# Softplus and the query mask on PSUM operands, feed-forward scales in the activation, the scan's source on GpSimd

## The chip, the cores and the metric

One core of one Trainium2 chip runs the whole program. The metric is the device time of one execution in microseconds; below that stand the span of the profiled execution (first to last instruction) and the granted TensorE clock. Everything is float32.

## The reference, cut to what matters

One decoder layer over 16 sequences of 64 tokens, width 128: a Mamba block (selective scan with 256 inner channels and 16 states), a cross attention with squared, L2-normalised scores (16 heads of 8), and a feed-forward of five scaled linear layers, each followed by a residual sum and a layer norm.

```python
xc = silu(causal_depthwise_conv(xm, conv_w, conv_b))
delta = jax.nn.softplus(dt @ W_dt + b_dt)
# for each token t: A is -exp(A_log), 256 channels x 16 states
h = jnp.exp(d_t[..., None] * A) * h + (d_t * u_t)[..., None] * B_t[:, None, :]
y = jnp.einsum('bdn,bn->bd', h, C_t)
...
qn = _l2_rownorm(q)
kn = _l2_rownorm(k)
scores = jnp.einsum('bhqd,bhkd->bhqk', qn, kn)
attn = scores * scores
...
h = jax.nn.silu(_tlin(x, w1_w, w1_s)) * _tlin(x, w2_w, w2_s)   # _tlin: (x @ w.T) * s, s per output column
h = jax.nn.gelu(_tlin(h, h1_w, h1_s), approximate=False)
h = jax.nn.gelu(_tlin(h, h2_w, h2_s), approximate=False)
return _tlin(h, w3_w, w3_s)
```

## The kernel before

The 1024 tokens are cut into four blocks (0 to 3) of 256. Channels or features lie on the 128 partitions and tokens along the free dimension, so a 256-channel tensor of a block is 128 x 2 x 256. Each engine works through a fixed list of steps, written out in `ORDER` (lines 86 to 144); a step is named `kind:block`, `kind:scan step` or the like, and an engine does its steps strictly in that order, waiting on semaphores inside each. So one late step holds all that stands behind it on its engine.

The selective scan is 32 scan steps, eight for each block, two states each. For step s: ScalarE writes the decays exp(delta*A) to PSUM (`decay_`, L897); GpSimd multiplies `du` (delta times the input) by B (`scan_in`, L1228); VectorE runs the recurrence (`scan`, L1091); GpSimd multiplies by C (`scan_out`, L429, in `out_product`). For blocks 0 and 1 TensorE sums the products (`mamba_sum`, L653), for blocks 2 and 3 VectorE does (`reduce`, L1108). Then `mamba_y` (L1141, L1145) applies the gate, and the block goes on through `gate_out`, `proj_out`, norm 1, the attention (`query`, `attend`, `attend_out`, `attn_out`), norm 2, and the feed-forward (`gate_up`, `hid1`, `hid2`, `down`, L745, L760, L771) and norm 3. B and C are written to DRAM as rows (`bc_store`) and fetched back broadcast over the partitions (`b_fetch`, `c_fetch`), by SyncE's DMA queue.

The places that the change touches:

- Softplus, stably, as max(v,0) + log(1+exp(-|v|)) with a correction for the rounding of 1+e. ScalarE writes |v| to `expo` in SBUF (L873), then exp(-|v|) over it (L879), then the log into the PSUM tile that held v (L882). VectorE computes `pre` = max(v,0) (L1064), then `rest` from `expo` by L1072 (one SBUF input) and L1074 (`expo` and `rest`, two SBUF inputs), then L1080 with the log from PSUM. `soft_end` on VectorE then writes `delta` (L406) and `du` = delta * xc (L410), each with two SBUF inputs.
- Query mask: ScalarE copies q with its bias to SBUF (L948), squares it (L951), and VectorE multiplies the SBUF copy by a head mask, 128 x 4 x 256 (`mask_queries`, L437).
- Scales: four rows of 512 are broadcast into `hid_a` and `hid_b` by two DMAs (`late:1`, L469). `fold:0` multiplies two of them into w1T and w2T (L1043, L1044); `fold:1` and `fold:2` multiply the other two into h1T and h2T (L1047, 128 x 2048 each). `gelu_layer` on ScalarE (L984) takes 512 columns in one instruction.
- Small scaled matrices: a diagonal of d_skip (L1032, two instructions) and the scaled centring matrix (L1037), both on VectorE.

Of the kernel before, what the change touches and what calls it, by code (L numbers as in the profile page):

```python
# [33 lines left out]
MASK_ON = ("dve", "dve", "dve", "dve")  # L34
# [23 lines left out]
        ("d_skip", CH), ("b_out_bo", 2), ("bq", 1), ("bk", 1), ("s3", 1), ("hmask", HI), ("early", SEQS * (TAPS - 1)), ("eps", 2)]  # L58
# [3 lines left out]
def columns(parts):  # L62
    at, n = {}, 0
    for name, w in parts:
# [11 lines left out]
    "front": (("xm",), ("delta",), ("bc",), ("soft",), ("soft_end",)),  # L76
# [16 lines left out]
        gate_up:0:0 gate_up:0:1 gate_out:1 key_norm:1 hid1:0:0 proj_out:1 norm_var:1:1 values:1 keys:2 query:1
        hid1:0:1 query_norm:1 attend:1:0 hid2:0:0 attend:1:1 hid2:0:1 attend_out:1 key_norm:2 gate_out:2 attn_out:1
        norm_var:1:2 down:0 norm_var:0:3 keys:3 gate_up:1:0 gate_up:1:1 proj_out:2 hid1:1:0 norm_var:2:1 hid1:1:1
        query:2 values:2 query_norm:2 hid2:1:0 attend:2:0 hid2:1:1 attend:2:1 gate_z:3 attend_out:2 attn_out:2
        key_norm:3 norm_var:2:2 down:1 gate_out:3 norm_var:1:3 proj_out:3 norm_var:3:1 gate_up:2:0 gate_up:2:1
        values:3 query:3 hid1:2:0 query_norm:3 attend:3:0 hid1:2:1 attend:3:1 hid2:2:0 attend_out:3 attn_out:3
        hid2:2:1 norm_var:3:2 down:2 norm_var:2:3 gate_up:3:0 gate_up:3:1 hid1:3:0 hid1:3:1 hid2:3:0 hid2:3:1 down:3
        norm_var:3:3  # L100
    """,
    "act": """
        prep xm:0 prep2 delta:0 soft:0 decay:0 decay:1 keys:0 xm:1 xm:2 decay:2 decay:3 delta:1 prep3 soft:1 decay:4
        decay:5 decay:6 gate_m:0 delta:2 soft:2 decay:7 centre_w decay:8 decay:9 decay:10 decay:11 xm:3 gate_m:1
        gate_m:2 gate_z:1 gate_z:0 decay:12 decay:13 delta:3 norm_var:0:1 soft:3 decay:14 norm_scale:0:1 query:0
        query_norm:0 decay:15 decay:16 keys:1 attend:0:0 skip:2 attend:0:1 decay:17 decay:18 norm_var:0:2
        norm_scale:0:2 decay:19 gate_m:3 gate_z:2 gate_up:0:0 gate_up:0:1 decay:20 decay:21 decay:22 hid1:0:0
        norm_var:1:1 norm_scale:1:1 keys:2 query:1 decay:23 hid1:0:1 query_norm:1 attend:1:0 decay:24 hid2:0:0
        attend:1:1 hid2:0:1 decay:25 decay:26 norm_var:1:2 decay:27 norm_scale:1:2 norm_var:0:3 norm_scale:0:3
# [10 lines left out]
        scan:10 mamba_y:0 fold:1 gate_out:0 scan:11 bc:3 scan:12 delta:3 soft:3 norm_apply:0:1 scan:13 scan:14  # L120
        query:0 values:0 scan:15 scan:16 soft_end:3 attend_out:0 scan:17 fold:2 norm_apply:0:2 mamba_y:1 scan:18
        scan:19 gate_up:0:0 gate_up:0:1 scan:20 scan:21 key_norm:1 gate_out:1 reduce:6 norm_apply:1:1 scan:22
        values:1 query:1 scan:23 reduce:7 reduce:8 mamba_y:2 scan:24 key_norm:2 attend_out:1 scan:25 scan:26
        gate_out:2 norm_apply:1:2 norm_apply:0:3 scan:27 gate_up:1:0 gate_up:1:1 reduce:9 norm_apply:2:1 scan:28
# [100 lines left out]
def decoder_layer(nc, xT, ctxT, mats, vecs, bv, cw, srow, scratch, out):  # L225
# [11 lines left out]
    with ExitStack() as ctx:  # L237
# [107 lines left out]
        def tile(key):  # L345
            return bank[home[key]]
# [956 lines left out]
```

## Time and profile before

| | us |
|---|---|
| median of three runs | 263.56 (263.06 to 264.9) |
| the profiled execution's own time | 262.27 |
| its span, first to last instruction | 260.4 |
| mean granted TensorE clock in it | 0.937 |

Times of single instructions come from that one profiled execution. Each engine has a row of its own; "idle before, releaser" is how long the engine stood still in front of an instruction and what ended it. A group's mean hides its spread where an instruction sometimes has to wait inside.

### The profile page before, as it was taken

The page shows a single profiled execution, that of the slowest core. Times are in us where ns is not written, and L with a number is a line of the kernel's source. Part 1 is how long each engine was busy: PE and PEld are TensorE (multiplying, and loading weights), DVE is VectorE, ACT ScalarE, POOL GpSimd, SP SyncE. Part 2 cuts the span into 40 slices and gives each one's busy share as a digit, 9 for nine tenths or more (in the row PEclk, how much of TensorE's full clock was granted, in tenths as well). Part 3 has the DMA queues.
Part 4 walks back from the last instruction along what each step waited for, and adds up shares of the span by engine and source line. Part 5 has one row for each costly group of instructions (what it writes and reads, how often), then busy time and mean ns, then how long its engine had stood idle before and what let it go on. Part 6 is the DMA issues. An engine that isn't in the chain of part 4 may idle for free.

```text
span 260.4 us, 3882 instructions
## 1 busy us (share of the span) xinstructions
PE 223.2 (86%) x1458; PEld 158.4 (61%) x1458; DVE 180.0 (69%) x153; ACT 160.3 (62%) x310; POOL 160.2 (62%) x71
## 2 busy tenths in 40 slices
PE   8999709956999967889869798899899899988992
PEld 6777404534667433348737577687667677776881
DVE  1234899999997989988989999799996250004000
ACT  4077925493858855719885869899874728154113
POOL 4004999699959999999999499999460000000000
PEclk9999976996899997599985999999999999999998
DMA  6749235962400540523314422350000000000000
GB/s 216 290 131 316 84 145 167 392 268 84 142 24 0 166 161 1 159 86 113 133 59 137 130 81 83 72 193 2 0 3 0 24 0 3 3 0 20 0 3 20
DMA packets 7269, 25.44 MB, mean 98 GB/s; under 512 B 977, under 2 KB 1746, under 8 KB 7122
## 3 DMA queue, kind: packets, MB, share of 16 engines
q1 hardware_dynamic: 7250, 25.18, 28.0%
q8 instruction: 12, 0.20, 0.3%
q14 instruction: 7, 0.06, 0.1%
HBM read 24.52 MB, written 0.66 MB: 97 GB/s over the span
## 4 chain that ended last, share of the span: by engine, by line
PE 33%; DVE 22%; issue 17%; POOL 14%; ACT 7%; DMA 5%; SPq 0%; DVEq 0%; POOLq 0%; ACTq 0%
PE work L760 13%; DVE state L1091 8%; POOL prod L429 7%; POOL state L1228 7%; PE work L563 4%; ACT L792 3%; DVE qmask L437 3%; DMA b_buf<-bc_scratch 2%; DVE rest L1074 2%; DMA cw_row<-cw 2%; PE work L653 2%; DVE prod L1108 2%; PE work L710 2%; PE work L686 2%; PE work L670 1%
## 5 line engine op out<-in xcount | busy, mean ns | idle before, releaser
L1228 POOL TENSOR_TENSOR state<-du,b_buf 128x1024 f32<-128x1024 f32 x32 | 82.1, 2586 | 19.7 <-DMA b_buf<-bc_scratch 19.7
L429 POOL TENSOR_TENSOR prod<-state,c_buf 128x1024 f32<-128x1024 f32 x32 | 76.4, 2407 | 12.4 <-DVE state L1091 6.0
L1091 DVE TENSOR_TENSOR_SCAN state<-decay,state 128x1024 f32<-128x1024 f32 x32 | 72.1, 2276 | 6.4 <-POOL state L1228 4.5
L897 ACT ACTIVATE decay<-delta,neg_a 128x252 f32<-128x252 f32 x128 | 52.5, 459 | 15.6 <-DVE state L1091 13.5
L653 PE MATMUL work<-prod,mat 128*128 128x512 f32 x64 | 35.0, 691 | 10.3 <-DVE mat L1032 7.8
L792 ACT ACT_TABLE_LOAD x31 | 39.8, 1283 | 1.3 <-PEq L1296 0.7
L760 PE MATMUL work<-hid_a,mat 128*128 128x256 f32 x128 | 30.3, 391 | 1.1 <-DVE hid_a L1201 0.9
L760 PE MATMUL work<-hid_b,mat 128*128 128x256 f32 x128 | 29.3, 383 | 0.0
L653 PEld LDWEIGHTS work<-prod,mat 128*128 128x128 f32 x64 | 13.5, 220 | 25.5 <-issue 12.3
L760 PEld LDWEIGHTS work<-hid_a,mat 128*128 128x128 f32 x128 | 24.8, 197 | 5.7 <-issue 1.7
L760 PEld LDWEIGHTS work<-hid_b,mat 128*128 128x128 f32 x128 | 23.9, 190 | 4.8 <-issue 1.5
L1108 DVE TENSOR_REDUCE prod<-prod 128x512 f32<-128x4096 f32 x4 | 17.6, 4412 | 2.0 <-POOL prod L429 2.0
L563 PE MATMUL work<-x,wf 128*128 128x256 f32 (+3 forms) x64 | 17.9, 428 | 0.2 <-DVE bf L1015 0.2
L1166 DVE TENSOR_TENSOR final<-work,root_ffn 128x256 f32<-128x256 f32 x4 | 1.7, 424 | 22.5 <-ACT root_ffn L942 22.5
L745 PE MATMUL work<-x,mat 128*128 128x256 f32 x64 | 15.1, 383 | 0.2 <-DVE final L1166 0.2
L563 PEld LDWEIGHTS work<-x,wf 128*128 128x128 f32 x64 | 13.3, 217 | 2.6 <-DMA x<-xT 0.7
L984 ACT ACTIVATE hid_a<-work 128x512 f32<-128x512 f32 x8 | 4.8, 597 | 14.5 <-PE work L760 14.5
L745 PEld LDWEIGHTS work<-x,mat 128*128 128x128 f32 x64 | 11.9, 190 | 2.7 <-issue 0.6
L437 DVE TENSOR_TENSOR qmask<-q,vec 128x1024 f32<-128x1024 f32 x4 | 13.3, 3334 | 0.0
L710 PE MATMUL work<-qmask,keys 32*64 32x256 f32 x128 | 8.8, 389 | 3.5 <-DVE qmask L437 2.4
L984 ACT ACTIVATE hid_b<-work 128x512 f32<-128x512 f32 x8 | 4.8, 596 | 11.4 <-PE work L760 11.4
L1189 DVE TENSOR_TENSOR mat<-work,rq 128x128 f32<-128x128 f32 x8 | 1.9, 277 | 14.1 <-PE work L726 14.1
(134 smaller groups left out, 327.6 us busy)
## 6 DMA issues: line engine op xcount, KB each, us to landing
b_buf<-bc_scratch SPq DMA_DIRECT2D x16, 512.0 KB, 4.1
c_buf<-bc_scratch SPq DMA_DIRECT2D x16, 512.0 KB, 4.0
mat<-mats SPq DMA_DIRECT2D x1, 2560.0 KB, 10.5
mat<-mats SPq DMA_DIRECT2D x1, 640.0 KB, 4.2
cw_row<-cw SPq DMA_DIRECT2D x1, 512.0 KB, 5.4
x<-xT SPq DMA_DIRECT2D x1, 512.0 KB, 6.2
kv<-ctxT SPq DMA_DIRECT2D x1, 512.0 KB, 8.1
hid_a<-srow SPq DMA_DIRECT2D x1, 512.0 KB, 11.3
```

The lines of the kernel that those rows point to most:

```text
L429: engine.tensor_tensor(products(b, n), slot(s), c_buf[c % C_RING][:, states, None, :].broadcast_to([P, SG, CH, T]), ALU.mult).then_inc(don ...
L437: engine.tensor_tensor(qmask[:, :, :], q[:, None, :].broadcast_to([P, HI, T]), v("hmask")[:, :, None].broadcast_to([P, HI, T]), ALU.mult). ...
L563: mm(o[:, :, late:], wf4[:, k, c * P:(c + 1) * P], xs[:, :, 0:SEQ - late], start=(late == 0), stop=False, skip_group_check=True)
L653: i = mm(tile(("y", b))[:, :], ident, products(b, n)[:, k, :, :].rearrange("p c t -> p (c t)"), start=(n == 0 and k == 0), stop=False, ski ...
L710: i = mm(tile(("s", b, g))[e * SEQ:(e + 1) * SEQ, p * HI * SEQ:(p + 1) * HI * SEQ], keysT[b % KEEP][r, t:t + SEQ], qmask[r, :, t:t + SEQ], ...
L745: i = mm(tile((key, b, j))[:, n * T:(n + 1) * T], m(w)[:, (2 * j + n) * P:(2 * j + n + 1) * P], x2[b % 2][:, :], start=True, stop=True)
L760: i = mm(tile((key, b, j))[:, n * T:(n + 1) * T], w[:, k, c:c + P], src[:, k, :], start=(k == 0), stop=(k == FT - 1))
L792: nc.scalar.preload_act_table_set(name)
L897: i = act_(decay[:, s % DA_RING, k, c, :].rearrange("p (s t) -> p s t", t=SEQ)[:, :, 1:], delta[b % KEEP][:, c, :].rearrange("p (s t) -> p ...
L1091: vec_.tensor_tensor_scan(h, decay[:, s % DA_RING, :, :, :].rearrange("p k c t -> p (k c t)"), h, 0.0, ALU.mult, ALU.add).then_inc(scanned, 1)
L1108: vec_.tensor_reduce(dst, src, axis=AX.XY, op=ALU.add).then_inc(reduced, 1)
L1228: nc.gpsimd.tensor_tensor(slot(s), du[b % KEEP][:, None, :, :].broadcast_to([P, SG, CH, T]), b_buf[c % B_RING][:, states, None, :].broadca ...
```

## The change

1. Softplus of blocks 1 to 3: exp(-|v|) goes into the PSUM tile that held v, not back to `expo` in SBUF, and L1072 and L1074 read it there. Since the log overwrites the same tile, ScalarE now waits for both of them before the log, and for `pre` before the exp. Block 0 stays as it was.
2. `soft_end` keeps only `delta`; `du` becomes a step of its own, on VectorE for block 0 and on GpSimd for blocks 1 to 3.
3. The query mask reads q from PSUM and adds the bias in the same VectorE instruction; ScalarE's SBUF copy of q is gone.
4. The scales of the second and third feed-forward layers are given to Gelu as per-partition scale, so each Gelu becomes two instructions of 256 columns; `fold:2` and both 2048-column products are gone (`fold:0` and `fold:1` now do w1T and w2T), and the second scale DMA too.
5. The diagonal and the scaled centring matrix are made on ScalarE (in `prep3`), not VectorE.
6. All five orders are written anew.

```diff
+DU_ON = ("dve", "pool", "pool", "pool")
...
+        def exponential(b):
+
+            return expo[:, :, :] if b == 0 else tile(("dl", b))[:, :].rearrange("p (c t) -> p c t", c=CH)
+
...
-            engine.tensor_tensor(delta[b % KEEP][:, :, :], pre[:, :, :], rest[:, :, :], ALU.add).then_inc(soft_step, 1)
-            eng.wait_ge(soft_step, 2 * b + 1)
+            engine.tensor_tensor(delta[b % KEEP][:, :, :], pre[:, :, :], rest[:, :, :], ALU.add).then_inc(delta_ready, 1)
+
+        def scan_source_of(eng, engine, b):
+
+            eng.wait_ge(delta_ready, b + 1)
             if b >= KEEP:
                 eng.wait_ge(in_ready, STEPS * (b - KEEP + 1))
-            engine.tensor_tensor(du[b % KEEP][:, :, :], delta[b % KEEP][:, :, :], xc[b % XC_KEEP][:, :, :], ALU.mult).then_inc(soft_step, 1)
+            engine.tensor_tensor(du[b % KEEP][:, :, :], delta[b % KEEP][:, :, :], xc[b % XC_KEEP][:, :, :], ALU.mult).then_inc(du_ready, 1)
...
+                act.wait_ge(loaded["win_z"], 16)
+                wait_filled(act, ("bfm",))
+                for c in range(CH):
+                    i = act_(diag[:, c, :], ident, ACT.Copy, scale=v("d_skip")[:, c:c + 1])
+                i.then_inc(diag_ready, 1)
+                act_(s3_centre[:, :], m("centre"), ACT.Copy, scale=v("s3")[:, 0:1]).then_inc(centre_ready, 1)
...
                 act.wait_ge(soft_act, 3 * b + 1)
-                act_(expo[:, :, :], expo[:, :, :], ACT.Exp, scale=-1.0).then_inc(soft_act, 1)
+                act.wait_ge(soft_max, b + 1)
+                e = exponential(b)
+                act_(e, expo[:, :, :], ACT.Exp, scale=-1.0).then_inc(soft_act, 1)
                 act.wait_ge(soft_act, 3 * b + 2)
-                act.wait_ge(soft_max, b + 1)
-                act_(tile(("dl", b))[:, :], expo[:, :, :].rearrange("p c t -> p (c t)"), ACT.Ln, bias=1.0).then_inc(soft_act, 1)
+                if b > 0:
+                    act.wait_ge(soft_rest, 2 * b + 2)
+                act_(tile(("dl", b))[:, :].rearrange("p (c t) -> p c t", c=CH), e, ACT.Ln, bias=1.0).then_inc(soft_act, 1)
...
-            engine.tensor_tensor(qmask[:, :, :], q[:, None, :].broadcast_to([P, HI, T]), v("hmask")[:, :, None].broadcast_to([P, HI, T]),
-                                 ALU.mult).then_inc(qm_ready, 1)
...
-                act_(q[:, :], tile(("q", b))[:, 0:T], ACT.Identity, bias=v("bq")).then_inc(q_ready, 1)
...
+                vec_.scalar_tensor_tensor(out=qmask[:, :, :], in0=tile(("q", b))[:, None, 0:T].broadcast_to([P, HI, T]), scalar=v("bq"),
+                                          in1=v("hmask")[:, :, None].broadcast_to([P, HI, T]), op0=ALU.add, op1=ALU.mult).then_inc(used["dve"], 1)
...
-                    act_(dst[:, 2 * j:2 * j + 2, :].rearrange("p n t -> p (n t)"), tile((key, b, j))[:, :], ACT.Gelu).then_inc(used["act"], 1)
+                    for n in range(2):
+                        i = act_(dst[:, 2 * j + n, :], tile((key, b, j))[:, n * T:(n + 1) * T], ACT.Gelu, scale=v(scale)[:, 2 * j + n:2 * j + n + 1])
+                    i.then_inc(used["act"], 1)
...
-                w = m(f"h{n}T").rearrange("p (k n) -> p k n", k=FT)
-                vec_.tensor_tensor(w, w, s_row[n + 1][:, None, :].broadcast_to([P, FT, HID]), ALU.mult).then_inc(folded, 1)
```

Of the new orders, the parts that the prediction speaks of: SyncE now fetches B and C of block 0 ahead of `late:0` (two weight loads) and puts `bc_store:1` behind `b_fetch:2`; TensorE does `xm:3` behind `mamba_sum:3`, with `mamba_sum:5` to `mamba_sum:7` close behind, and `gate_up:2:0 gate_up:2:1` ahead of `gate_out:3` (before: behind `proj_out:3` and `norm_var:3:1`); GpSimd's `du:1` stands between `scan_in:6` and `scan_in:7`, `du:2` ahead of `scan_out:11`, `du:3` ahead of `scan_in:24`; VectorE does

```
reduce:10 norm_apply:2:2 reduce:11 norm_apply:1:3 mamba_y:3 gate_up:2:0 gate_up:2:1 gate_out:3
```

where before it was `reduce:10 attend_out:2 reduce:11 mamba_y:3 norm_apply:2:2 key_norm:3 gate_out:3`, with `gate_up:2` three steps later.

## Rows read from the trace of the kernel before

**Rows 1.** The page's head and busy time by engine, whole span.
```profile
span 260.4 us, 3882 instructions
...
PE 223.2 (86%) x1458; PEld 158.4 (61%) x1458; DVE 180.0 (69%) x153; ACT 160.3 (62%) x310; POOL 160.2 (62%) x71
```

**Rows 2.** Windows: start:end, us; busy PE, PEld, DVE, ACT, POOL; clock; DMA.
```profile
60.00:160.00 100.00, 87.79 (x592) 58.01 (x593) 92.56 (x66) 68.32 (x139) 93.57 (x38) 0.88 0.30 101
160.00:199.00 39.00, 35.52 (x301) 27.62 (x300) 35.77 (x25) 33.22 (x63) 29.27 (x13) 1.00 0.15 45
199.00:260.40 61.40, 54.01 (x382) 42.35 (x380) 11.24 (x22) 24.86 (x41) 0.00 (x0) 0.98 0.02 8
```

**Rows 3.** Groups of GpSimd: busy us, mean ns of one, idle before and releasers.
```profile
L1228 POOL TENSOR_TENSOR state<-du,b_buf 128x1024 f32<-128x1024 f32 x32 | 82.1, 2586 | 19.7 <-DMA b_buf<-bc_scratch 19.7
L429 POOL TENSOR_TENSOR prod<-state,c_buf 128x1024 f32<-128x1024 f32 x32 | 76.4, 2407 | 12.4 <-DVE state L1091 6.0 <-issue 3.4 <-PE work L653 3.0
```

**Rows 4.** Timeline of GpSimd: start, us, instruction, [idle before]; first and idle ones.
```profile
23.00 9.28 POOL L1228 TENSOR_TENSOR state<-du,b_buf 128x1024 f32<-128x1024 f32 x4 [19.74 <-DMA b_buf<-bc_scratch]
...
49.09 5.11 POOL L429 TENSOR_TENSOR prod<-state,c_buf 128x1024 f32<-128x1024 f32 x2 [2.36 <-DVE state L1091]
...
74.44 2.35 POOL L429 TENSOR_TENSOR prod<-state,c_buf 128x1024 f32<-128x1024 f32 x1 [3.02 <-PE work L653]
...
149.25 2.38 POOL L429 TENSOR_TENSOR prod<-state,c_buf 128x1024 f32<-128x1024 f32 x1 [3.42 <-issue]
...
188.21 4.69 POOL L429 TENSOR_TENSOR prod<-state,c_buf 128x1024 f32<-128x1024 f32 x2 [3.41 <-DVE state L1091]
```

**Rows 5.** Groups of VectorE that the change touches, and one with a PSUM input.
```profile
L437 DVE TENSOR_TENSOR qmask<-q,vec 128x1024 f32<-128x1024 f32 x4 | 13.3, 3334 | 0.0
L1074 DVE TENSOR_TENSOR rest<-expo,rest 128x512 f32<-128x512 f32 x4 | 8.9, 2214 | 0.1
...
L410 DVE TENSOR_TENSOR du<-delta,xc 128x512 f32<-128x512 f32 x4 | 6.8, 1708 | 0.1
...
L406 DVE TENSOR_TENSOR delta<-pre,rest 128x512 f32<-128x512 f32 x4 | 6.2, 1560 | 0.0
...
L1197 DVE SCALAR_TENSOR_TENSOR hid_a<-up,work 128x512 f32<-128x512 f32 x8 | 5.4, 680 | 2.9 <-ACT up L974 2.9
L1047 DVE TENSOR_TENSOR mat<-mat,hid_b 128x2048 f32<-128x2048 f32 x2 | 5.3, 2636 | 0.0
...
L1072 DVE TENSOR_SCALAR rest<-expo 128x512 f32<-128x512 f32 x4 | 4.9, 1228 | 0.0
...
L1032 DVE TENSOR_SCALAR mat<-mat,vec 128x128 f32<-128x128 f32 x2 | 3.2, 1650 | 0.0
...
L1037 DVE TENSOR_SCALAR s_centre<-mat,vec 128x128 f32<-128x128 f32 x1 | 1.5, 1521 | 0.0
```

**Rows 6.** Timeline of VectorE: softplus of block 0, and the mask of block 1.
```profile
18.51 0.42 DVE L1072 TENSOR_SCALAR rest<-expo 128x512 f32<-128x512 f32 x1
18.96 0.69 DVE L1074 TENSOR_TENSOR rest<-expo,rest 128x512 f32<-128x512 f32 x1
...
21.31 0.69 DVE L410 TENSOR_TENSOR du<-delta,xc 128x512 f32<-128x512 f32 x1
...
141.62 5.30 DVE L437 TENSOR_TENSOR qmask<-q,vec 128x1024 f32<-128x1024 f32 x1
```

**Rows 7.** Timeline of ScalarE: a pair of 256 columns, and the last Gelu.
```profile
194.14 0.84 ACT L862 ACTIVATE zgate<-work,half_bz 128x256 f32<-128x256 f32 x2
...
252.96 0.60 ACT L984 ACTIVATE hid_a<-work 128x512 f32<-128x512 f32 x1 [2.86 <-PE work L760]
```

**Rows 8.** Timeline: SyncE's weight loads, VectorE's last gated y, TensorE's gate_up of block 2.
```profile
15.73 0.90 SPq L444 DMA_DIRECT2D mat<-mats  x2
...
197.74 0.69 DVE L1145 TENSOR_TENSOR yg<-mat,mgate 128x512 f32<-128x512 f32 x1
...
204.57 3.81 PE L745 MATMUL work<-x,mat 128*128 128x256 f32 x16
```

More of the change, by code:

```diff
@@ L75 @@
 LANES = {
-    "front": (("xm",), ("delta",), ("bc",), ("soft",), ("soft_end",)),
+    "front": (("xm",), ("delta",), ("bc",), ("soft",), ("soft_end",), ("du",)),
     "gates": (("gate_m",), ("gate_z",)),
@@ L93 @@
[L93 to L97, printed above, removed]
@@ L98 @@
-        values:3 query:3 hid1:2:0 query_norm:3 attend:3:0 hid1:2:1 attend:3:1 hid2:2:0 attend_out:3 attn_out:3
-        hid2:2:1 norm_var:3:2 down:2 norm_var:2:3 gate_up:3:0 gate_up:3:1 hid1:3:0 hid1:3:1 hid2:3:0 hid2:3:1 down:3
-        norm_var:3:3
+        prep xm:0 prep2 bc:0 delta:0 prep3 xm:1 xm:2 keys:0 bc:1 bc:2 delta:1 key_norm:0 mamba_sum:0 mamba_sum:1
+        gate_m:0 gate_m:1 mamba_sum:2 mamba_sum:3 centre_w delta:2 xm:3 mamba_sum:4 gate_m:2 mamba_sum:5 mamba_sum:6
+        mamba_sum:7 gate_z:1 gate_z:0 gate_out:0 bc:3 centre_b delta:3 proj_out:0 norm_var:0:1 values:0 query:0
@@ L101 @@
+        query:2 values:2 query_norm:2 attend:2:0 attend:2:1 hid2:1:0 hid2:1:1 attend_out:2 gate_z:3 attn_out:2
+        norm_var:2:2 down:1 norm_var:1:3 gate_up:2:0 gate_up:2:1 gate_out:3 proj_out:3 hid1:2:0 norm_var:3:1
+        hid1:2:1 key_norm:3 query:3 query_norm:3 values:3 attend:3:0 attend:3:1 hid2:2:0 attend_out:3 hid2:2:1
+        attn_out:3 norm_var:3:2 down:2 norm_var:2:3 gate_up:3:0 gate_up:3:1 hid1:3:0 hid1:3:1 hid2:3:0 hid2:3:1
+        down:3 norm_var:3:3
     """,
     "act": """
-        prep xm:0 prep2 delta:0 soft:0 decay:0 decay:1 keys:0 xm:1 xm:2 decay:2 decay:3 delta:1 prep3 soft:1 decay:4
@@ L120 @@
[L120 to L124, printed above, removed]
@@ L125 @@
-        scan:29 values:2 query:2 scan:30 scan:31 reduce:10 attend_out:2 reduce:11 mamba_y:3 norm_apply:2:2
-        key_norm:3 gate_out:3 norm_apply:1:3 norm_apply:3:1 gate_up:2:0 gate_up:2:1 values:3 query:3 attend_out:3
-        norm_apply:3:2 norm_apply:2:3 gate_up:3:0 gate_up:3:1 norm_apply:3:3
+        prep bc:0 delta:0 soft:0 soft_end:0 du:0 scan:0 scan:1 scan:2 prep3 bc:1 bc:2 scan:3 delta:1 soft:1
+        soft_end:1 scan:4 key_norm:0 scan:5 scan:6 scan:7 scan:8 delta:2 soft:2 scan:9 mamba_y:0 scan:10 fold:0
@@ new lines @@
+        centre_b bc:3 soft_end:2 gate_out:0 scan:11 scan:12 delta:3 norm_apply:0:1 values:0 soft:3 query:0 fold:1
+        scan:13 scan:14 scan:15 scan:16 scan:17 soft_end:3 attend_out:0 mamba_y:1 scan:18 norm_apply:0:2 scan:19
+        gate_out:1 gate_up:0:0 gate_up:0:1 scan:20 scan:21 norm_apply:1:1 reduce:6 query:1 key_norm:1 values:1
+        scan:22 scan:23 reduce:7 reduce:8 attend_out:1 mamba_y:2 scan:24 norm_apply:1:2 scan:25 gate_out:2 scan:26
+        norm_apply:0:3 gate_up:1:0 gate_up:1:1 key_norm:2 scan:27 scan:28 scan:29 norm_apply:2:1 query:2 values:2
@@ L128 @@
+        reduce:9 scan:30 scan:31 attend_out:2 reduce:10 norm_apply:2:2 reduce:11 norm_apply:1:3 mamba_y:3
+        gate_up:2:0 gate_up:2:1 gate_out:3 norm_apply:3:1 key_norm:3 query:3 values:3 attend_out:3 norm_apply:3:2
+        norm_apply:2:3 gate_up:3:0 gate_up:3:1 norm_apply:3:3
     """,
     "pool": """
-        scan_in:0 scan_in:1 scan_in:2 scan_in:3 scan_out:0 scan_out:1 scan_in:4 scan_in:5 scan_out:2 scan_out:3
-        scan_out:4 scan_out:5 scan_in:6 scan_in:7 scan_in:8 scan_in:9 scan_out:6 scan_out:7 scan_in:10 scan_out:8
@@ L195, in emptied_in @@
         return [("y", *at)] if SUM_ON[at[0]] == "pe" else []
[L196 removed]
+    one = {"soft": "dl", "query": "q", "bc": "bc", "key_norm": "ssk", "values": "v", "gate_out": "oi"}
     if kind in one:
```

154 lines of the change are left out of this document (70 added, 84 removed).

## The prediction

> **What bounds the kernel now.** I read the busy times first [rows 1]. TensorE is busy most (86%), but no engine is full, so the average decides nothing. I then read the windows [rows 2] and cut at about 199 us, where the gated y of the last block is ready (197.74 + 0.69 = 198.43 [rows 8]). In the 100 us from 60 to 160, GpSimd is busy 93.6 and VectorE 92.6; TensorE has 87.8, at a mean clock of 0.88. After 199 GpSimd does nothing, VectorE 11 of 61, and TensorE is busy 54.0 of 61.4. So there are two stages: a scan stage paced by GpSimd and VectorE together, and a tail of 260.4 - 198.43 = 62.0 us paced by TensorE and the last block's chain of dependences.
>
> GpSimd's scan stage adds up. It begins at 23.00 and its last two instructions end at 188.21 + 4.69 = 192.90 [rows 4], 169.9 us. An undisturbed one takes 9.28 / 4 = 2.32 us [rows 4], and 64 of them 148.5. It stood idle 12.4 us inside the stage [rows 3]. The remaining 9.0 us are stretching, visible as means of 2586 and 2407 ns against 2320 [rows 3]. Stretching goes both ways. L1074 takes 0.69 us for block 0, before GpSimd has started [rows 6], yet has a mean of 2214 ns [rows 5]; that is about 0.69 plus one GpSimd instruction. The mask of block 1 took 5.30 [rows 6]. L1197, of the same size but with one input in PSUM, has a mean of 680 ns [rows 5] though half of its eight fall in the scan stage.
>
> **The change part by part, on VectorE.**
> - Mask: 13.3 us for four [rows 5]. The new one has its 1024 elements in PSUM. Twice L1197's 0.68 bounds it above at 1.36; L1197's own 0.68, for half the columns, is the lower end. I take 1.25, nearest to the upper: 5.0 in all, 8.3 less.
> - L1074: 8.9 becomes 4 x 0.69 = 2.8, 6.1 less. L1072: 4.9 becomes 0.42 (block 0 [rows 6]) + 3 x 0.68 = 2.5, 2.4 less; 0.68 is L1197 again, and the present mean of 1228 ns is the upper end. Undisturbed, as in block 0, L1072 takes 0.42 and L1074, of the same size, 0.69 [rows 6]; the three that move were disturbed, their mean is (4.9 - 0.42) / 3 = 1.49. The Trainium skill has a rule against this part (VectorE: DVE Perf Modes, "Why PSUM operands drop a tier"): a single fp32 source in SBUF is read at double rate, one in PSUM is not, so against an undisturbed 0.42 the move would cost 3 x 0.26 = 0.8 us and not save 2.4. By that rule alone VectorE's sum below would be 3.2 us smaller; by the rows the 0.42 is not what the three instructions get beside GpSimd.
> - The log now stands behind L1074, so VectorE waits for it in front of L1080: one ScalarE pass of 512 columns, 0.60 [rows 7], and the hand-over, some 0.8 each, 2.4 for three. Bounds: 0 (other steps can't come between, so a gain is excluded) to 1.5 each. Behind the waiting exp and log on ScalarE stand the decays, for which the scans wait; the decays run at most two scan steps ahead.
> - `du` of blocks 1 to 3 off VectorE: 6.8 - 0.69 = 6.1 less. The two 2048-column folds: 5.3 less. Diagonal and centring matrix: 3.2 + 1.5 = 4.7 less.
>
> Sum on VectorE: 8.3 + 6.1 + 2.4 - 2.4 + 6.1 + 5.3 + 4.7 = 30.5 us less, nearly all before 199.
>
> **On GpSimd.** Three `du` are added, unseen there before. They are half the size of L429, so 1.16 each; bounds 0.69 (VectorE's) and 2.32 (a whole one). I take 3.5 in all. The start: `du:0` is ready at 21.31 + 0.69 = 22.0 [rows 6], the first B landed at 23.0 [rows 4] behind two weight loads issued at 15.73 [rows 8]. These loads now go later, so GpSimd starts at about 22.0. The four idle times [rows 4]: 2.36 waited for a scan that stood behind softplus, diagonal and centring matrix on VectorE, and goes; 3.42 and 3.41 are scans behind masks (the mask at 141.62 holds VectorE for 5.30 us [rows 6], and GpSimd's next product comes at 149.25), and go mostly; 3.02 waited for sums on TensorE behind `xm:3`, and the new order does these closer. I leave 4 of the 12.4 for what comes late next: the summing of blocks 2 and 3 on VectorE, and decays behind the log. Of the 9.0 of stretching I leave 3, for the three `delta` instructions (L406, still two SBUF inputs, mean 1560) and a few others like them.
>
> GpSimd's end: 22.0 + 148.5 + 3.5 + 4 + 3 = 181.0. From its end to the gated y it was 198.43 - 192.90 = 5.5 us (two sums, one product), kept: 186.5.
>
> **On TensorE.** No large matmul group changes. From 60 to 199 it did 87.8 x 0.88 + 35.5 = 112.8 us of work in terms of the full clock [rows 2], and `gate_up:2`, 3.8 [rows 8], now comes before the y too: 116.6. Having started the stage some 3 us sooner, it has 186.5 - 57 = 129.5 us, a share of 90%. The best it showed in the scan stage is 35.5 of 39, 91% at clock 1.00 [rows 2]. It can just do it, with no room for its own waits, so I add 2.5 us: gated y at 189.0.
>
> **On ScalarE.** 16 Gelus become pairs: 0.84 - 0.60 = 0.24 each [rows 7], 3.8 us; three small copies come, four copies of q go. All lies beside TensorE's work, ScalarE being busy 62%. In the tail only the last Gelu's 0.24 could show, and the residual matmul and first half of `down` cover it. If that cover went it would be 0.24 for each of four, 1.0.
>
> **The tail.** 62.0 now. `gate_up:2` moves in front of the y (minus 3.5 to 3.8). In its place VectorE has the four products of `gate_up:2`, 4 x 0.68 = 2.7, between `mamba_y:3` and `gate_out:3`, beside 1.8 us of TensorE's `gate_out:3`: plus 1. With 0.5 for Gelu and for the mask's new wait for the squares: 60.0.
>
> **Sum.** Span 189.0 + 60.0 = 249.0. The profiled time is 1.87 above its span (262.27 - 260.4), and the median of the runs 1.29 above the profiled time: 252.2 us, 11.4 less than 263.56.
>
> **The rivals.**
> - TensorE takes the bound (0.25). Of the 139 us from 60 to 199 it lost 139 - 112.8 = 26.2 to waits and clock. If 22 of these stay, because they are latencies of norms and of the attention and not GpSimd's fault, the y comes at 57 + 116.6 + 22 = 195.6, and the time is 195.6 + 60 + 3.2 = 258.8. For it: 91% from 160 on. Against: waits of TensorE for masks and softplus are among those that go.
> - All stalls go (0.08): neither the 4 idle, nor 2 of the stretching, nor the 2.5 of TensorE: 8.5 less, 243.7.
> - It doesn't do what it says (0.05): an input in PSUM does not free the instruction while its other input and output lie in SBUF. Then mask and softplus stay long. Two mask stalls (6.8) come back and 3 us of stretching, 262.0. Against it stands L1197's even 680 ns.
> - Slower than before (0.04): TensorE's clock. It was 0.88 from 60 to 160, where its gaps were long, and 0.98 to 1.00 after [rows 2]. If the reordered tail has longer gaps and falls to 1.2 GHz, each us of matmul there costs another. The forecast has 11.4 us in hand, so from 14 of the tail's 54 us on it is more than 1% slower; at 18, 270.2 us. Nothing in the tail before shows such a fall for long.
>
> **How the numbers follow.** The forecast has 0.58; its own range is 247 to 256. A measurement of this kernel tells about 1% from no change, 260.9 to 266.2. Faster by more: 0.58 + 0.08, nearly all of the first rival (0.23) and a part of the third (0.01) = 0.90. Within 1%: 0.06. Slower: 0.04. The range reaches up to the TensorE rival and down to half of the way to the stall-free case: 246.5 to 259.
>
> **What would show it.** Right: L1072, L1074 and the mask near 0.68, 0.69 and 1.25 us in the scan stage; GpSimd's `du` at about 1.2; L1228 and L429 with means within 60 ns of 2320; GpSimd ending near 181, gated y of block 3 near 189, tail near 60, TensorE's clock over 0.9 from 60 on. Wrong: scans idle for decays by more than 5 us in all (the log's new wait), GpSimd idle for `du`, or TensorE's y and attention steps running late while VectorE idles.

## The result and the profile after

The executions of the changed kernel took 250.69, 264.64, 250.61 and 265.29 us; those of the kernel before on the same chip have a median of 263.31 (261.57 to 264.9). The changed kernel's median is 257.66. The ratio of 0.952, 95% interval 0.942 to 0.962, leaves out executions more than 1.5% above a kernel's fastest, and so the two of 265 us; why the changed kernel has such executions is the main question of the experiments.

The profiled execution took 250.69 us. Page's head and windows (start:end, us; busy PE, PEld, DVE, ACT, POOL; clock; DMA), cut at 187, between GpSimd's end and the gated y:

```profile
span 248.8 us, 3892 instructions
...
PE 215.0 (86%) x1458; PEld 154.4 (62%) x1458; DVE 153.9 (62%) x145; ACT 165.4 (66%) x327; POOL 157.0 (63%) x74
```

```profile
60.00:160.00 100.00, 87.93 (x618) 59.08 (x619) 84.09 (x72) 75.84 (x155) 97.20 (x43) 0.95 0.32 108
160.00:187.00 27.00, 24.42 (x256) 19.31 (x255) 23.33 (x15) 23.55 (x47) 20.46 (x9) 1.00 0.07 23
187.00:248.80 61.80, 53.29 (x380) 41.97 (x378) 12.33 (x23) 28.41 (x49) 0.00 (x0) 1.00 0.02 7
```

Against [rows 1, 2]: VectorE has lost 26 us of work, GpSimd fills 97.2 of the 100 us from 60 to 160 (before 93.6), and TensorE's clock there went from 0.88 to 0.95. GpSimd is now the pacer alone. Its groups (busy, mean ns, idle before), answering to [rows 3]:

```profile
L1226 POOL TENSOR_TENSOR state<-du,b_buf 128x1024 f32<-128x1024 f32 x32 | 77.0, 2424 | 20.0 <-DVE du L417 19.5 <-POOL prod L435 0.2
L435 POOL TENSOR_TENSOR prod<-state,c_buf 128x1024 f32<-128x1024 f32 x32 | 75.0, 2365 | 4.3 <-DVE state L1086 2.5 <-DMA c_buf<-bc_scratch 1.9
L417 POOL TENSOR_TENSOR du<-delta,xc 128x512 f32<-128x512 f32 x3 | 3.8, 1268 | 0.6 <-DVE delta L410 0.6
```

Idle inside the stage fell from 12.4 to 5.1 us (4.3 + 0.2 + 0.6), the means from 2586 and 2407 ns. VectorE's groups, answering to [rows 5]:

```profile
L410 DVE TENSOR_TENSOR delta<-pre,rest 128x512 f32<-128x512 f32 x4 | 9.4, 2362 | 0.1
...
L1177 DVE SCALAR_TENSOR_TENSOR qmask<-work,vec 128x1024 f32<-128x1024 f32 x4 | 5.1, 1284 | 4.1 <-ACT q L951 4.1
...
L1071 DVE SCALAR_TENSOR_TENSOR rest<-work,log_one,rest 128x512 f32<-128x512 f32 x4 | 3.0, 751 | 2.3 <-ACT work L885 2.1
...
L1063 DVE TENSOR_SCALAR rest<-work 128x512 f32<-128x512 f32 x3 | 2.1, 692 | 1.7 <-ACT work L881 1.6
L1065 DVE TENSOR_TENSOR rest<-work,rest 128x512 f32<-128x512 f32 x3 | 2.1, 692 | 0.1
```

Everything that now has an operand in PSUM runs at one even duration. `delta`, the old L406, which still has two SBUF inputs, got worse, from a mean of 1560 to 2362 ns. The last products of GpSimd and the last gated y:

```profile
177.77 4.70 POOL L435 TENSOR_TENSOR prod<-state,c_buf 128x1024 f32<-128x1024 f32 x2 [2.01 <-DVE state L1086]
```

```profile
188.19 0.68 DVE L1140 TENSOR_TENSOR yg<-mat,mgate 128x512 f32<-128x512 f32 x1
```

GpSimd ends at 182.47 (before 192.90), the y is there at 188.87 (198.43), and the tail is 248.8 - 188.87 = 59.9 (62.0).

### The profile page after: what moved, and what is told of

Same layout as the page of the kernel before. It is cut to its first block, busy times and chain, and to the rows that moved or that the text cites. A ratio compares the mean times of both kernels' runs of the same rounds, so it can differ in the third digit from the quotient of the medians.

```text
span 248.8 us, 3892 instructions
## 1 busy us (share of the span) xinstructions
PE 215.0 (86%) x1458; PEld 154.4 (62%) x1458; DVE 153.9 (62%) x145; ACT 165.4 (66%) x327; POOL 157.0 (63%) x74
## 4 chain that ended last, share of the span: by engine, by line
PE 50%; DVE 20%; ACT 18%; issue 8%; POOL 1%; DMA 1%; DVEq 0%; ACTq 0%; POOLq 0%
PE work L754 12%; PE work L648 9%; DVE state L1086 9%; ACT L786 4%; ACT decay L900 4%; PE work L558 3%; PE work L765 3%; PE work L705 2%; PE work L681 2%; PE work L721 2%; DVE prod L1103 2%; PE work L512 2%; PE work L596 2%; PE work L665 1%; PE work L740 1%
## 5 line engine op out<-in xcount | busy, mean ns | idle before, releaser
L1226 POOL TENSOR_TENSOR state<-du,b_buf 128x1024 f32<-128x1024 f32 x32 | 77.0, 2424 | 20.0 <-DVE du L417 19.5
L435 POOL TENSOR_TENSOR prod<-state,c_buf 128x1024 f32<-128x1024 f32 x32 | 75.0, 2365 | 4.3 <-DVE state L1086 2.5
L648 PE MATMUL work<-prod,mat 128*128 128x512 f32 x64 | 30.4, 622 | 0.1
L648 PEld LDWEIGHTS work<-prod,mat 128*128 128x128 f32 x64 | 12.4, 199 | 14.0 <-issue 13.0
L558 PE MATMUL work<-x,wf 128*128 128x256 f32 (+3 forms) x64 | 15.6, 385 | 1.2 <-ACT wouto_wo_c L839 1.2
L983 ACT ACTIVATE hid_b<-work,vec 128x256 f32<-128x256 f32 x16 | 6.6, 471 | 11.1 <-PE work L754 11.1
L1170 DVE SCALAR_TENSOR_TENSOR x<-work,b_centred,root_attn 128x256 f32<-128x256 f32 x8 | 3.8, 474 | 16.2 <-ACT root_attn L945 16.2
L558 PEld LDWEIGHTS work<-x,wf 128*128 128x128 f32 x64 | 11.5, 189 | 3.2 <-issue 1.5
L934 ACT ACTIVATE sq_attn<-work,b_centred 128x256 f32<-128x256 f32 x8 | 3.7, 468 | 14.4 <-PE work L732 8.1
L983 ACT ACTIVATE hid_a<-work,vec 128x256 f32<-128x256 f32 x16 | 6.6, 471 | 6.7 <-PE work L754 6.6
L410 DVE TENSOR_TENSOR delta<-pre,rest 128x512 f32<-128x512 f32 x4 | 9.4, 2362 | 0.1
```

The costliest lines, as they stand in the source:

```text
L410: engine.tensor_tensor(delta[b % KEEP][:, :, :], pre[:, :, :], rest[:, :, :], ALU.add).then_inc(delta_ready, 1)
L435: engine.tensor_tensor(products(b, n), slot(s), c_buf[c % C_RING][:, states, None, :].broadcast_to([P, SG, CH, T]), ALU.mult).then_inc(don ...
L558: mm(o[:, :, late:], wf4[:, k, c * P:(c + 1) * P], xs[:, :, 0:SEQ - late], start=(late == 0), stop=False, skip_group_check=True)
L648: i = mm(tile(("y", b))[:, :], ident, products(b, n)[:, k, :, :].rearrange("p c t -> p (c t)"), start=(n == 0 and k == 0), stop=False, ski ...
L983: i = act_(dst[:, 2 * j + n, :], tile((key, b, j))[:, n * T:(n + 1) * T], ACT.Gelu, scale=v(scale)[:, 2 * j + n:2 * j + n + 1])
L1226: nc.gpsimd.tensor_tensor(slot(s), du[b % KEEP][:, None, :, :].broadcast_to([P, SG, CH, T]), b_buf[c % B_RING][:, states, None, :].broadca ...
```

## The experiments

The texts that stood on record before each run speak of theories. The port theory: VectorE instructions with two SBUF inputs and GpSimd's instructions hold each other up, and the gain comes from having fewer of the former. The order theory: it comes from the new orders. The starvation theory, from the folds' run on: such an instruction can stay locked out over several GpSimd instructions, and that makes the long executions.

Times are of whole executions. Beside each group of runs the kernel before had a median between 262.4 and 263.8 us.

**The changed kernel once more.** No edit.

> The changed kernel as it is, beside the kernel before on one chip, as the yardstick for the other runs. Both theories: span within 1 us of 248.8 where TensorE's mean granted clock is near 0.965; near 263 where it is near 0.92.

250.96, 265.52, 264.45 and 261.38 us. So three of its eight executions lie between 250.6 and 251.0, five between 261.4 and 265.5, and none in the 10 us between. Over all eight the median is 262.9, no better than the kernel before (262.4 and 263.3 beside these two groups). The profile is again of the short group (span 249.1), and one instruction in it differs from the first in a way that matters later: `delta:1`, two SBUF inputs, in the first profile and in this one:

```profile
44.64 4.09 DVE L410 TENSOR_TENSOR delta<-pre,rest 128x512 f32<-128x512 f32 x1
```

```profile
45.69 1.79 DVE L410 TENSOR_TENSOR delta<-pre,rest 128x512 f32<-128x512 f32 x1
```

GpSimd beside the first:

```profile
43.52 2.36 POOL L435 TENSOR_TENSOR prod<-state,c_buf 128x1024 f32<-128x1024 f32 x1
45.82 2.36 POOL L1226 TENSOR_TENSOR state<-du,b_buf 128x1024 f32<-128x1024 f32 x1
48.81 1.26 POOL L417 TENSOR_TENSOR du<-delta,xc 128x512 f32<-128x512 f32 x1 [0.63 <-DVE delta L410]
```

In the first it waited over the end of one GpSimd instruction and the whole next one, and ended at 48.73, 0.55 after GpSimd's end at 48.18, with GpSimd standing still. In the second it got in at the first boundary.

**The new orders alone.** The code of before with all five new orders; `du` stays inside `soft_end`, and `fold:2` stands behind `fold:1`.

```diff
-        prep bc:0 delta:0 soft:0 soft_end:0 scan:0 scan:1 scan:2 bc:1 scan:3 prep3 delta:1 soft:1 prep2 scan:4
+        prep bc:0 delta:0 soft:0 soft_end:0 scan:0 scan:1 scan:2 prep3 prep2 bc:1 bc:2 scan:3 delta:1 soft:1
...
+        centre_b bc:3 soft_end:2 gate_out:0 scan:11 scan:12 delta:3 norm_apply:0:1 values:0 soft:3 query:0 fold:1 fold:2
...
```

> The kernel before with the new orders, and no other part of the change (its du stays inside soft_end, both 2048-column folds stay, behind the query of block 0). Port theory (the gain comes from taking VectorE work out that GpSimd has to share a port with): most of the gain is gone, span 257 to 262, and the mask and L1074 again have means over 2000 ns. Order theory (the gain is the new order of TensorE's and SyncE's steps): span 250 to 254.

269.67 to 271.97 us, ratio 1.029 (1.022 to 1.037): slower than before, which no theory had expected. GpSimd's products now wait for scans (groups, as above):

```profile
L428 POOL TENSOR_TENSOR prod<-state,c_buf 128x1024 f32<-128x1024 f32 x32 | 77.1, 2425 | 21.5 <-DVE state L1090 19.6 <-DMA c_buf<-bc_scratch 1.0 <-issue 0.5
```

The longest, 8.45 us, ends at 108.76; ahead of it VectorE did a mask and then the two 2048-column folds (4.5 us from 101.94) while scans queued behind them. The orders carry none of the gain by themselves, and both theories' spans were missed.

**The parts alone.** The changed kernel's code with the orders of before (`du:1` to `du:3` on GpSimd ahead of `scan_in:8`, `:16`, `:24`).

```diff
-        scan_out:8 scan_out:9 scan_in:11 scan_in:12 scan_in:13 scan_out:10 scan_in:14 du:2 scan_out:11 scan_in:15
+        scan_in:11 scan_in:12 scan_out:9 scan_out:10 scan_out:11 scan_in:13 scan_in:14 scan_out:12 scan_in:15 du:2
...
```

> The changed kernel with the orders of before; du of blocks 1 to 3 stands on GpSimd right ahead of the block's first scan_in. Port theory: a good half of the gain is there, span 252 to 256, with GpSimd's idle time inside the scan stage under 8 us (12.4 before). Order theory: span 258 to 262.

250.93 to 253.6 us in every execution, ratio 0.961 (0.952 to 0.969). GpSimd idles 4.9 us in the stage at means of 2414 and 2390 ns. So the gain is in the parts (the text above expected a good half of it), and none of these four executions is long. By the medians, 253.28 against 262.9, the new orders made the change worse, not better.

**Mask from SBUF.** Of the changed kernel only the mask is undone.

```diff
+                act_(q[:, :], tile(("q", b))[:, 0:T], ACT.Identity, bias=v("bq")).then_inc(q_ready, 1)
...
-                vec_.scalar_tensor_tensor(out=qmask[:, :, :], in0=tile(("q", b))[:, None, 0:T].broadcast_to([P, HI, T]), scalar=v("bq"),
-                                          in1=v("hmask")[:, :, None].broadcast_to([P, HI, T]), op0=ALU.add, op1=ALU.mult).then_inc(used["dve"], 1)
+                vec_.tensor_tensor(qmask[:, :, :], q[:, None, :].broadcast_to([P, HI, T]), v("hmask")[:, :, None].broadcast_to([P, HI, T]),
+                                   ALU.mult).then_inc(qm_ready, 1)
```

> The changed kernel with only the query mask as before: q copied to SBUF by ScalarE, the mask from two SBUF inputs. Port theory: the three masks inside the scan stage take 2.3 to 5.3 us each, the fourth, after GpSimd's end, 1.2; the span is 2 to 6 us longer than the changed kernel's 248.8. Order theory: the masks have slack in the new order, under 1 us longer.

258.63, 262.57, 268.75 and 271.11 us. The shortest is 8.0 above the changed kernel's shortest, more than the 2 to 6 expected. In the profile only one of the four masks is long, 3.95 us at 142.64 (the others 1.22, 1.37 and 1.22), so their own length does not explain the 8 us. That profile (span 266.9) is of a long execution, and in its timeline stands something that the mask has no part in. VectorE, GpSimd and TensorE around 72 us:

```profile
71.84 11.59 DVE L1039 SCALAR_TENSOR_TENSOR mat<-mat,hid_a 128x512 f32<-128x512 f32 x1
```

```profile
73.62 6.97 POOL L1230 TENSOR_TENSOR state<-du,b_buf 128x1024 f32<-128x1024 f32 x3
80.53 2.36 POOL L436 TENSOR_TENSOR prod<-state,c_buf 128x1024 f32<-128x1024 f32 x1
83.03 2.60 POOL L1230 TENSOR_TENSOR state<-du,b_buf 128x1024 f32<-128x1024 f32 x1
```

```profile
86.83 1.22 PE L671 MATMUL work<-x,mat 128*128 128x256 f32 x2 [11.04 <-DVE mat L1154]
```

`fold:0`, two SBUF inputs and 0.68 us of work, took 11.59. GpSimd's instructions follow each other here without a gap (each line begins before the one above has ended) until 80.53 + 2.36 = 82.89. There it stands still for 0.14 us, and the fold ends at 83.43, 0.54 later. In the short execution of the changed kernel the same fold got in at the first boundary between two GpSimd instructions:

```profile
71.99 1.73 DVE L1035 SCALAR_TENSOR_TENSOR mat<-mat,hid_a 128x512 f32<-128x512 f32 x1
```

```profile
73.13 7.87 POOL L1226 TENSOR_TENSOR state<-du,b_buf 128x1024 f32<-128x1024 f32 x3
```

Behind the fold on VectorE stand `delta:2`, the product after the gate's matmul, for which TensorE waited 11.04 us, and the scans. Window 80 to 100 of the long execution, its first 6.8 us still inside that wait:

```profile
80.00:100.00 20.00, 7.73 (x17) 4.40 (x17) 15.66 (x16) 5.58 (x13) 16.10 (x8) 0.51 0.26 80
```

TensorE was busy 7.73 of 20 us and its granted clock 0.51, about the lower of its levels (1.2 GHz). From 87 to 107, with work again (busy 14.54 us), the clock was still 0.50; the short execution has 0.74 from 80 to 100. That gave a theory with a test: it is the new order of GpSimd (`scan_in:11`, `:12`, `:13`, `scan_out:10` without a gap where VectorE has the fold and `delta:2`) that makes the two groups.

**Folds on GpSimd.** The changed kernel with w1T and w2T scaled on GpSimd behind `du:2`, ScalarE halving w1T before. This is the base of the next four.

```diff
+            def fold(n):
...
+                w = m(("w1T", "w2T")[n])
+                nc.gpsimd.tensor_tensor(w, w, s_row[n], ALU.mult).then_inc(folded, 1)
```

> The changed kernel with the two products that fold the scales into w1T and w2T moved from VectorE to GpSimd, behind du:2 (ScalarE halves w1T). Starvation theory (in the long executions of the changed kernel VectorE's first fold, which has two SBUF inputs, waits some 10 us for GpSimd to leave a gap, as the 11.59 us fold in the profile of the kernel with the old mask): every execution lies within 249 to 254 us. Rival (those executions are long because the chip grants TensorE less clock, whatever VectorE does): again some near 250 and some at 262 or more.

251.91, 254.55, 256.64, 258.16, 258.66 and 263.2 us. The expected 249 to 254 us held for one of six. The two groups became a spread, median 257.4: the fold was not the only cause, it happened to stand there. `delta:2` stands there too.

**The base with the mask from SBUF** (the edit of the mask above).

```diff
-                vec_.scalar_tensor_tensor(out=qmask[:, :, :], in0=tile(("q", b))[:, None, 0:T].broadcast_to([P, HI, T]), scalar=v("bq"),
+                vec_.tensor_tensor(qmask[:, :, :], q[:, None, :].broadcast_to([P, HI, T]), v("hmask")[:, :, None].broadcast_to([P, HI, T]),
...
```

> The previous kernel with only the query mask as before, from two SBUF inputs. Starvation and port theory: no execution over 260; 1 to 5 us longer than the previous kernel, as masks inside the scan stage take up to 4 us in place of 1.28. Order theory: under 1 us longer.

262.57 to 271.01 us, against the base's 251.9 to 263.2: the gain is gone, and the forecast (none over 260) is missed. The masks inside the scan stage take 3.25, 3.96 and 3.37 us (1.28 in the base), and `delta:2` is starved, so the profile does not separate the two:

```profile
74.37 9.02 DVE L412 TENSOR_TENSOR delta<-pre,rest 128x512 f32<-128x512 f32 x1
```

```profile
73.61 6.94 POOL L1230 TENSOR_TENSOR state<-du,b_buf 128x1024 f32<-128x1024 f32 x3
80.51 2.33 POOL L437 TENSOR_TENSOR prod<-state,c_buf 128x1024 f32<-128x1024 f32 x1
82.98 2.61 POOL L1230 TENSOR_TENSOR state<-du,b_buf 128x1024 f32<-128x1024 f32 x1
```

The end is at 83.39, 0.55 after GpSimd's 82.84. In the base the same instruction stood almost the same way to GpSimd (0.79 us behind the start of its three products, here 0.76) and got in at the next boundary:

```profile
74.09 2.11 DVE L411 TENSOR_TENSOR delta<-pre,rest 128x512 f32<-128x512 f32 x1
```

```profile
73.30 7.42 POOL L1226 TENSOR_TENSOR state<-du,b_buf 128x1024 f32<-128x1024 f32 x3
```

**The base with softplus in SBUF**, on the old waits.

```diff
-            return expo[:, :, :] if b == 0 else tile(("dl", b))[:, :].rearrange("p (c t) -> p c t", c=CH)
+            return expo[:, :, :]
```

> The same kernel with only the softplus as before: exp(-|v|) in SBUF for all blocks, with the waits of before. Port theory: L1072's and L1074's successors take 1.2 to 2.7 us each beside GpSimd, 7 us of VectorE in all, partly paid back by a log that waits less; 1 to 5 us longer. Rival (the new wait of the log costs as much as the port did): the same within 1 us or shorter.

252.28 to 256.14 us, ratio 0.963 (0.955 to 0.971). The two instructions that had been moved are long again for blocks 1 to 3 (0.69, 1.83, 0.43, and 2.72 three times), but the waits for the exp and the log (1.6 and 2.1 us in the base) are gone, and the y comes at 190.06 against 189.70 of the base. So the moved softplus is worth about 0.4 us in the profiles, as the rival had it. By the medians, 254.4 against the base's 257.4, it may even cost something: without it no execution reaches 258 us. The waits of scans for decays are 4.9 us in both profiles, so the new waits on ScalarE do not lengthen those.

**The base with `du` on VectorE.**

```diff
-DU_ON = ("dve", "pool", "pool", "pool")
+DU_ON = ("dve", "dve", "dve", "dve")
```

> The same kernel with du of all four blocks on VectorE, right behind delta. Port theory: three more instructions with two SBUF inputs, 0.7 to 2.7 us each, against 3.8 us less on GpSimd: between 2 us shorter and 3 us longer, with more spread. Rival (GpSimd alone sets the pace of the scan stage): 3 to 4 us shorter.

254.13 to 256.73 us, ratio 0.969 (0.963 to 0.975). Three `du` of 2.72 us each, y at 191.90, 2.2 later than in the base. Against the base's profile this is 2.2 us longer, by the medians (255.4 and 257.4) 2.0 shorter; the spread of 2.6 us is smaller, not larger as expected.

**`delta` from PSUM.** If the starved instruction is the cause, taking its second SBUF input away must cure the spread. On the base, for blocks 1 and 2, L1071 writes its sum back to the log's PSUM tile and `delta` reads it there, right behind softplus. That puts `delta:2` ahead of `scan:9`, so its place changes too, and the run does not tell the operand from the place.

```diff
+LATE_SUM = (1, 2)
...
+            src = tile(("dl", b))[:, :].rearrange("p (c t) -> p c t", c=CH) if b in LATE_SUM else rest[:, :, :]
+            i = engine.tensor_tensor(delta[b % KEEP][:, :, :], src, pre[:, :, :], ALU.add)
...
+                vec_.scalar_tensor_tensor(out=log if b in LATE_SUM else rest[:, :, :], in0=log, scalar=log_one[:, 0:1], in1=rest[:, :, :],
```

> The changed kernel with no VectorE instruction of two SBUF inputs left between 45 and 100 us: the folds on GpSimd, and for blocks 1 and 2 the sum with the log written back to PSUM, from which delta is made right behind it. Starvation theory: every execution between 248 and 254 us, none over 257. Rival (the long executions are the chip's, or come from the two waits on TensorE and ScalarE in the new order): again a spread of 10 us or more.

250.85 to 251.22 in four of six, the others 253.74 and 255.68 (one over the 254 expected, none over 257); median 251.16, ratio 0.954 (0.949 to 0.959). Nothing at 261 to 265 is left. `delta:1` and `delta:2` take 0.69 each, `delta:3`, still from SBUF, 2.85. It beats the kernel before by 12.5 us and the changed one's medians by 6.5 and more.

**The same on the orders of before**, with the folds on GpSimd and then on VectorE.

```diff
-        scan_in:11 scan_in:12 scan_out:9 scan_out:10 scan_out:11 scan_in:13 scan_in:14 scan_out:12 scan_in:15 du:2
+        scan_in:11 scan_in:12 scan_out:9 scan_out:10 scan_out:11 scan_in:13 scan_in:14 scan_out:12 scan_in:15 du:2 fold:0 fold:1
```

> The same edits on the kernel that has the change's parts and the orders of before. Starvation theory: every execution between 247 and 253 us, as that kernel had 250.9 to 253.6 with delta and folds contending; 2.5 us of folds are added on GpSimd, some 5 us of contention go.

260.37 to 264.58 us in all twelve executions, median 262.98: a clear miss, 11 us over the expected. The timelines of VectorE and GpSimd show the same lock-out at another place, on the one `delta` that still has two SBUF inputs:

```profile
103.21 12.08 DVE L420 TENSOR_TENSOR delta<-rest,pre 128x512 f32<-128x512 f32 x1
```

```profile
100.86 4.67 POOL L452 TENSOR_TENSOR prod<-state,c_buf 128x1024 f32<-128x1024 f32 x2
105.48 2.36 POOL L1242 TENSOR_TENSOR state<-du,b_buf 128x1024 f32<-128x1024 f32 x1
107.80 2.35 POOL L452 TENSOR_TENSOR prod<-state,c_buf 128x1024 f32<-128x1024 f32 x1
110.11 4.63 POOL L1242 TENSOR_TENSOR state<-du,b_buf 128x1024 f32<-128x1024 f32 x2
121.76 2.37 POOL L452 TENSOR_TENSOR prod<-state,c_buf 128x1024 f32<-128x1024 f32 x1 [7.02 <-PE work L665]
```

GpSimd ran out of work at 114.74, `delta:3` ended at 115.29, 0.55 later. It had waited over five GpSimd instructions. The pacer then stood still for 7.02 us, for a sum of TensorE (L665). In TensorE's order that sum stood behind a matmul that waited for VectorE's product right behind `delta:3`:

```profile
115.74 1.22 PE L749 MATMUL work<-mat,wouto_wo_c 128*128 128x256 f32 x2 [5.23 <-DVE mat L1203]
```

One execution of the twelve was profiled; that the others are long for the same reason is inferred. The folds on VectorE again:

```diff
-        scan_in:11 scan_in:12 scan_out:9 scan_out:10 scan_out:11 scan_in:13 scan_in:14 scan_out:12 scan_in:15 du:2 fold:0 fold:1
+        scan_in:11 scan_in:12 scan_out:9 scan_out:10 scan_out:11 scan_in:13 scan_in:14 scan_out:12 scan_in:15 du:2
```

> As the previous one, but with the two folds on VectorE, at the places of the orders of before. If contention of these two costs more than 2.5 us of GpSimd: longer than the previous one by 1 to 3 us, and a spread above 3 us; if it costs less, 1 to 2.5 us shorter.

252.83 to 256.56 us, median 254.75, ratio 0.965 (0.960 to 0.970). Two more instructions with two SBUF inputs on VectorE, and 8 us less, where the text above allowed 2.5. In the profile `delta:3` now gets in:

```profile
101.61 2.85 DVE L419 TENSOR_TENSOR delta<-rest,pre 128x512 f32<-128x512 f32 x1
```

```profile
99.26 4.66 POOL L451 TENSOR_TENSOR prod<-state,c_buf 128x1024 f32<-128x1024 f32 x2
103.88 2.82 POOL L1242 TENSOR_TENSOR state<-du,b_buf 128x1024 f32<-128x1024 f32 x1
```

Both `delta:3` began 2.35 us after the first of two products; one got the next boundary, the other none.

**A break in GpSimd's row of work.** The changed kernel with `du:2`, which must wait for `delta:2`, moved three steps forward: GpSimd has to stand still early if VectorE is held up.

```diff
-        scan_out:8 scan_out:9 scan_in:11 scan_in:12 scan_in:13 scan_out:10 scan_in:14 du:2 scan_out:11 scan_in:15
+        scan_out:8 scan_out:9 scan_in:11 scan_in:12 du:2 scan_in:13 scan_out:10 scan_in:14 scan_out:11 scan_in:15
```

> The changed kernel with one word of GpSimd's order moved: du:2 from behind scan_in:14 to behind scan_in:12. GpSimd then stops there until VectorE's fold and delta of block 2 are done, about 3 us into the stretch in which the long executions lost 10 us. Starvation theory (a VectorE instruction with two SBUF inputs that loses the port once gets it only when GpSimd stands still): every execution between 249 and 256 us, since the wait is cut to about 5 us where it occurs and costs nothing where it doesn't. Rival (the long executions have another cause): again some of six executions over 261 us.

250.64, 253.69, 254.42, 254.49, 255.57 and 257.75 us, median 254.45: five of six inside the 249 to 256 expected, none over 258, where the changed kernel has five of eight over 261. In the profile of the longest (span 255.9) the fold is locked out and let in as soon as GpSimd waits:

```profile
74.12 7.00 DVE L1035 SCALAR_TENSOR_TENSOR mat<-mat,hid_a 128x512 f32<-128x512 f32 x1
```

```profile
75.93 4.64 POOL L1226 TENSOR_TENSOR state<-du,b_buf 128x1024 f32<-128x1024 f32 x2
82.19 1.26 POOL L417 TENSOR_TENSOR du<-delta,xc 128x512 f32<-128x512 f32 x1 [1.62 <-DVE delta L410]
```

Its end, 81.12, is again 0.55 after GpSimd's 80.57, and `delta:2` behind it took 0.67.

## Why the prediction was right, and what it lacked

Of the profiled execution nearly each term came out as worked:

- **Mask, softplus, `du`.** The mask took 1.28 us (forecast 1.25), L1063 and L1065 0.69 each (0.68, 0.69), GpSimd's `du` 1.27 (1.16). An input in PSUM does free the instruction; that rival's premise fell. Undoing the mask alone brings back 8.0 us (shortest against shortest; 10.7 on the base), more than any other single edit tried. How much of that is the masks' own length is not shown: in both profiles another instruction is locked out too.
- **The wait for the log** cost VectorE 0.7 us three times, 2.1 (2.4). A second wait was in no term: the exp now waits for `pre`, and VectorE for the exp, 0.8 us each before two of the three L1063. The softplus edit as a whole is worth only the 0.4 us measured: it was priced in VectorE's busy time, and VectorE was not what paced the stage afterwards. Scans waited for decays 4.2 us in all, under the 5 named as wrong.
- **VectorE's sum** was too large: without the log's wait the forecast is 30.5 + 2.4 = 32.9 us less of busy time, the page of the profile says 26.1. The missing part is mostly in the instructions that kept two SBUF inputs: `delta` grew by 3.2 (9.4 against 6.2), the two 512-column folds from 1.4 to 2.5, yg's L1140 from 1.6 to 2.4. That these now meet a GpSimd that pauses less is the likely reason; of `delta`'s 3.2 us, 2.3 are the one wait at 44.64, which the second profile doesn't have. The end didn't suffer, since VectorE was no longer the pacer: its scans waited 7.5 us for GpSimd (4.5 before).
- **GpSimd.** Start 22.75 (22.0: the exp of block 0 now waits for `pre` too, and `du:0` ends 0.67 later; 23.81 in the second profile), idle 5.1 (4), stretching 182.47 - 22.75 - 148.5 - 3.8 - 5.1 = 2.3 (3), end 182.47 (181.0). Start and idle, each about 1 us late, make up the 1.5.
- **TensorE.** y at 188.87 (189.0), clock 0.95 from 60 on. 24.42 of the 27 us before 187 were busy, 90% at full clock. It did not take the bound: the y came 188.87 - 182.47 = 6.4 us behind GpSimd's end, 0.9 more than the 5.5 kept from before, where that rival had it at 195.6. Some luck is in the 189.0: GpSimd ended 1.5 late, and the 2.5 added for TensorE came to 0.9.
- **Tail.** 59.9 (60.0) at clock 1.00; the clock rival fell. The last Gelu pair took the 0.84 us foreseen. The Gelu edit wasn't run by itself, nor were the tail's order, the dropped 2048-column folds, or the move of the diagonal and centring matrix.
- **Span** 248.8 (249.0), the execution 250.69 (250.9).

The step that was wrong is the last: 1.29 us from the profiled execution to the median. It holds for the kernel before, whose 44 executions lie within 2.3% of each other (259.29 to 265.22). The changed kernel has a second group 10 to 15 us above, so its median of four is 257.66, 5.5 over the forecast of 252.2 and inside the range for a reason that stood in no rival. That it lies inside is luck: with two short and two long executions the median falls between the groups, where no execution lies, and the median of all eight, 262.9, is above the range. The lower bound also has a slip: half of the way from 252.2 to the stall-free 243.7 is 248.0, not 246.5. The stretching was priced as "0.69 plus one GpSimd instruction", 3.01 us; the three L1074 took 2.72 or 2.73 each, and that is only the usual case. The trace of before already had the other in it: the mask at 141.62 [rows 6] ended at 146.92, and GpSimd had stood still since 145.84, 1.08 us before; the mask had waited over two of its instructions, not one. I put the 5.30 us down as stretching and didn't ask what ended it.

What is shown: in four profiles of variants a VectorE instruction with two SBUF inputs waits 7 to 12 us and ends 0.54 or 0.55 us after GpSimd stands still. In all fourteen profiles together nine such instructions that began over 0.1 us ahead of a boundary between GpSimd instructions let at least that one pass, `delta:1` of the changed kernel among them, and all nine ended only behind a pause of GpSimd (0.14 to 7.02 us). In the changed kernel an early stop of GpSimd alone takes away every execution over 258 us (six executions); so does the PSUM input, with the folds and the place of `delta:2` moved. What is not shown: no profile was had of a 265-us execution of the changed kernel itself, so that its long ones come about in the same way is inferred from these. What decides at a boundary who comes in also stays open, since nearly equal offsets (0.76 and 0.79; 2.35 and 2.35; `delta:1` 1.12 and 1.10 behind the start of GpSimd's product) gave both outcomes.

## What to carry to other kernels

Give VectorE one PSUM operand wherever it works beside a busy GpSimd, even if a single undisturbed instruction gets slower (0.42 to 0.69 here): the gain is that in no profile here was such an instruction held up. Where an instruction with two SBUF inputs must stay, don't put it beside a long unbroken row of GpSimd instructions, or place in that row a step that waits for it. And try an edit on the orders of before as well: here the change's parts gave 250.9 to 253.6 us on them, without the long executions of the new orders, though with the next edits the old orders met a lock-out too (260.4 to 264.6 us). And take more than one execution before reading a profile as the kernel's time: here the profiled one was of the short group both times, and the longer group was the larger.

## What of the hardware was not expected

- **A lock-out over several instructions.** Fold 11.59 us over the rest of one GpSimd instruction and four whole ones, `delta:3` 12.08, `delta:2` 9.02, fold 7.00. The Trainium skill (SBUF — State Buffer, "Who interferes with whom") says that a VectorE instruction with two SBUF inputs contends with a GpSimd instruction that reads SBUF. The Trainium skill (same page, "SBUF: two separate sides") says that whichever of the two starts first gets the shared pair of ports for the whole instruction and the other fully blocks. The rows agree in that L1063, L1065 and the mask, with at most one SBUF input, stay at 0.69 and 1.28. That the wait is over with the instruction that came first they do not bear out: it can last until GpSimd pauses, and 0.14 us of pause were enough.
- **Chance.** The same program took 250.6 and 265.5 us in different executions, on one core.
- **Its price grows down the line.** The fold's 11.59 us held TensorE for 11.04, and for the 20 us after that its granted clock was 0.50.
